# The value matmuls of a block issued as two halves of 256 columns, one behind every two pairs of scores

## The reference

```
xn = layernorm(x)                         # x: 2 x 2048 x 256
q, k, v = split(xn @ w_qkv.T)             # 16 heads of 16
q, k = rope(q), rope(k)
attn = softmax(q @ k.T / 4)               # 2048 x 2048 for each of 32 batch and head
s = (attn @ v) @ w_out.T
g = silu(expert_ffn(xn))                  # each token to one of 8 experts
out = x + s * g
```

## Time and profile before

| | |
|---|---|
| time, median of 3 runs | 1651.2 us (1650.79 to 1651.39) |
| the profiled execution | 1654.93 us, its span 1653.2 us |
| mean granted TensorE clock | 0.976 |
| TensorE matmul busy | 1539.2 us, 93% |
| VectorE busy | 1367.1 us, 83% |
| ScalarE busy | 1189.0 us, 72% |
| GpSimd busy | 141.1 us, 9% |

### The profile page before, as it was taken

One profiled execution on the slowest core, in us unless ns is written; L12 is line 12 of the kernel. 1 busy time (PEld: TensorE's weight loads), 2 busy tenths in 40 slices (PEclk: granted clock), 3 DMA queues, 4 the chain that ended last, 5 costly groups with the idle time before them and its releaser, 6 DMA issues.

```text
span 1653.2 us, 29704 instructions
## 1 busy us (share of the span) xinstructions
PE 1539.2 (93%) x9121; PEld 660.2 (40%) x9121; DVE 1367.1 (83%) x1563; ACT 1189.0 (72%) x2381; POOL 141.1 (9%) x160
## 2 busy tenths in 40 slices
PE   6897999989899999999999999999999999999998
PEld 4453333346433333333333333333333333333336
DVE  7678799964599999999999999999999999999705
ACT  4452377855677787787788778778777877877780
POOL 2232322100122100000010000000010000000100
PEclk9998599989899999999999999999999999999999
DMA  5673234425444324222222242222222422222303
GB/s 199 226 193 117 55 78 100 67 48 154 103 78 78 61 42 93 42 42 42 39 40 41 39 90 39 39 41 41 41 42 42 90 39 39 41 40 35 62 4 118
DMA packets 77820, 116.54 MB, mean 70 GB/s; under 512 B 29072, under 2 KB 64272, under 8 KB 70800
## 3 DMA queue, kind: packets, MB, share of 16 engines
q1 hardware_dynamic: 69632, 101.89, 31.9%
q0 software_dynamic: 3072, 8.39, 2.0%
q10 hardware_dynamic: 5072, 5.72, 1.0%
HBM read 75.31 MB, written 39.85 MB: 70 GB/s over the span
## 4 chain that ended last, share of the span: by engine, by line
PE 74%; ACT 17%; DVE 3%; issue 3%; DMA 2%; SPq 1%; ACTq 0%; POOLq 0%; DVEq 0%
PE ps L1114 31%; PE ps L1103 31%; ACT arena L582 16%; PE ps L1035 3%; PE ps L1193 2%; PE ps L1036 1%; PE ps L1094 1%; PE ps L1209 1%; PE ps L1239 1%; DVE arena L692 1%; PE ps L1059 1%; DMA arena<-xs_d 1%; PE ps L1166 1%; PE ps L1046 1%; DMA out<-arena 1%
## 5 line engine op out<-in xcount | busy, mean ns | idle before, releaser
L726 DVE TENSOR_REDUCE arena<-ps 128x1 f32<-128x1024 f32 x992 | 1174.1, 1219 | 127.3 <-PE ps L1094 119.2
L582 ACT ACTIVATE arena<-ps 128x512 f32<-128x512 f32 x2048 | 1059.7, 603 | 275.3 <-PE ps L1103 274.1
L1103 PE MATMUL ps<-qs,ks 50*128 50x512 f32 x2048 | 754.5, 449 | 61.0 <-ACT arena L582 29.5
L1094 PE MATMUL ps<-ks,qs 48*128 48x512 f32 x1984 | 796.3, 474 | 4.3 <-DVE arena L726 2.5
L1103 PEld LDWEIGHTS ps<-qs,ks 50*128 50x128 f32 x2048 | 341.9, 186 | 685.6 <-issue 436.2
L1114 PE MATMUL ps<-arena 128*32 128x512 f32 x4096 | 551.6, 611 | 0.8 <-ACT arena L582 0.8
L1094 PEld LDWEIGHTS ps<-ks,qs 48*128 48x128 f32 x1984 | 331.9, 187 | 48.0 <-DVE arena L726 17.0
L1114 PEld LDWEIGHTS ps<-arena 128*32 128x32 f32 x4096 | 80.9, 108 | 130.3 <-ACT arena L582 113.7
L969 POOL COPY arena<-v_sb 128x256 f32 (+1 forms) x32 | 13.3, 416 | 1108.1 <-ACT arena L574 1090.8
L1035 PE MATMUL ps<-arena 128*128 128x512 f32 x128 | 68.8, 620 | 0.7 <-ACT arena L496 0.7
L692 DVE TENSOR_REDUCE arena<-ps 128x1 f32<-128x1024 f32 x32 | 39.1, 1222 | 23.8 <-PE ps L1059 23.8
(11 more groups left out here) (103 smaller groups left out, 543.0 us busy)
## 6 DMA issues: line engine op xcount, KB each, us to landing
qs<-parts_d SPq DMA_DIRECT2D x186, 128.0 KB
ks<-parts_d SPq DMA_DIRECT2D x186, 128.0 KB
parts_d<-arena SPq DMA_DIRECT2D x64, 256.0 KB, 2.6
xs_d<-arena SPq DMA_DIRECT2D x13, 384.0 KB, 3.4
arena<-xs_d SPq DMA_DIRECT2D x13, 384.0 KB, 3.8
ys_d<-arena SPq DMA_DIRECT2D x13, 384.0 KB, 2.8
onum_d<-arena SPq DMA_DIRECT2D x128, 32.0 KB
out<-arena ACTq DMA_DIRECT2D x16, 256.0 KB, 2.1
```

Of the source, the lines that this page charges most:

```text
L582: nc.scalar.activation(prob[kb % 2][:, c * W:(c + 1) * W], ps[:, bank, :], ACT.Exp, scale=SCALE).then_inc(exp_done[bank], 1)
L726: nc.vector.tensor_reduce(most[head_slot][:, tile, u:u + 1], ps[:, AB + 2 * u:AB + 2 + 2 * u, :], AX.XY, ALU.max).then_inc(a_reduced[u], 1)
L1094: ins = nc.tensor.matmul(ps[:, AB + c, :], qs[head_slot][ABASE:ABASE + KR, tile * P:(tile + 1) * P].bitcast(F32R), ks[head_slot][ABASE:ABA ...
L1103: nc.tensor.matmul(ps[:, bank, :], ks[s][0:KS, kb * P:(kb + 1) * P].bitcast(F32R), qs[s][0:KS, c * W:(c + 1) * W].bitcast(F32R), start=Tru ...
```

## The change

The value group is issued in two halves: columns 0 to 255 of all four column groups, then columns 256 to 511. A block is now: B scores c = 0 and 1 of the next block with their A scores, first half of the values of this block, B scores c = 2 and 3 of the next block with their A scores, second half. So score c = 3 moves from the start of its own block to the block before. The first half waits for all of the block's exponentials. `pv_done` is given by the second half. The wait for the next head's loads stands ahead of score c = 0 of block 15. All four scores of the very first block are issued ahead. Ahead of the expert part one score (c = 3 of the next head) is held back and issued behind it; for this pair 1 is written out on its own behind a loop that holds only pair 0.

```
--- before.py
+++ after.py
@@ -1103,18 +1103,21 @@
                 nc.tensor.matmul(ps[:, bank, :], ks[s][0:KS, kb * P:(kb + 1) * P].bitcast(F32R),
                                  qs[s][0:KS, c * W:(c + 1) * W].bitcast(F32R), start=True, stop=True).then_inc(scored[bank], 1)
 
-            def weigh_values(pi, s, kb):
-
-                if kb == 0:
+            def weigh_values(pi, s, kb, half):
+
+                if kb == 0 and half == 0:
                     pe.wait_ge(v_staged[s], pi + 1)
                     pe.wait_ge(o_out[1 - s], past(pi + s))
-                for c in range(1, QT):
-                    pe.wait_ge(exp_done[b_bank(s, kb, c)], past(b_before(pi, s, kb, c) + 1))
+                if half == 0:
+                    for c in range(1, QT):
+                        pe.wait_ge(exp_done[b_bank(s, kb, c)], past(b_before(pi, s, kb, c) + 1))
+                lo, hi = half * W // 2, (half + 1) * W // 2
                 for c in range(QT):
-                    last = nc.tensor.matmul(ps[32 * c:32 * (c + 1), PVB, :], vst[s][:, kb, :],
-                                            prob[kb % 2][:, c * W:(c + 1) * W],
-                                            start=(kb == 0), stop=(kb == KB - 1))
-                last.then_inc(pv_done[kb % 2], 1)
+                    last = nc.tensor.matmul(ps[32 * c:32 * (c + 1), PVB, lo:hi], vst[s][:, kb, :],
+                                            prob[kb % 2][:, c * W + lo:c * W + hi],
+                                            start=(kb == 0 and half == 0), stop=(kb == KB - 1 and half == 1))
+                if half:
+                    last.then_inc(pv_done[kb % 2], 1)
 
             pe.wait_ge(pt_out, NT)
             pe.wait_ge(qkv_out, NT)
@@ -1129,12 +1132,13 @@
             pe.wait_ge(counts_out, 1)
             pe.wait_ge(loaded[0], 16 * LOADS)
             pe.wait_ge(shift_loaded[0], 64)
-            for c in range(QT - 1):
+            for c in range(QT):
                 score(0, 0, 0, c)
 
-            def pair(pi, last_pair):
+            def pair(pi, last_pair, hold=False):
                 for s in range(2):
                     for kb in range(KB):
+                        held_back = hold and s == 1 and kb == KB - 1
                         g = pi * (2 * KB) + (s * KB + kb)
                         ahead = kb + AHEAD - KB
                         with_a = not last_pair or (s == 0 and ahead < KB)
@@ -1143,17 +1147,16 @@
                         b_slot, b_pi = (s, pi) if kb < KB - 1 else (1 - s, pi + s)
                         if with_a and ahead % KB == 0:
                             pe.wait_ge(a_loaded[a_slot], (pi + 2) * (16 * LOADS))
+                        if with_b and kb == KB - 1:
+                            pe.wait_ge(loaded[b_slot], (pi + 1 + s) * (16 * LOADS))
+                            pe.wait_ge(shift_loaded[b_slot], (pi + 1 + s) * 64)
                         for c in range(QT):
-                            if c == 0:
-                                score(pi, s, kb, QT - 1)
-                            elif with_b:
-                                if c == 1 and kb == KB - 1:
-                                    pe.wait_ge(loaded[b_slot], (pi + 1 + s) * (16 * LOADS))
-                                    pe.wait_ge(shift_loaded[b_slot], (pi + 1 + s) * 64)
-                                score(b_pi, b_slot, (kb + 1) % KB, c - 1)
+                            if with_b and not (held_back and c == QT - 1):
+                                score(b_pi, b_slot, (kb + 1) % KB, c)
                             if with_a:
                                 score_a(g + AHEAD, a_slot, ahead % KB, c)
-                        weigh_values(pi, s, kb)
+                            if c % 2:
+                                weigh_values(pi, s, kb, c // 2)
 
             def turn_sorted(i):
 
@@ -1212,9 +1215,11 @@
                 pe.wait_ge(inter_out, NF)
                 pe.wait_ge(y_out, NF)
 
-            with pe.Fori(0, FB) as pi:
+            with pe.Fori(0, FB - 1) as pi:
                 pair(pi, False)
+            pair(FB - 1, False, hold=True)
             experts()
+            score(FB, 0, 0, QT - 1)
             with pe.Fori(FB, NP - 1) as pi:
                 pair(pi, False)
             pair(NP - 1, True)
```

## The result

The changed kernel takes 1763.2 us (median; its runs lie between 1758.2 and 1798.8) against 1651.3: ratio 1.070, 95% interval 1.063 to 1.077. The forecast was 1596 us, with a range of 1582 to 1642. The profiled execution is the longest, 1798.8 us, 36 us over the median, so what it shows as the price of a stall is more than the median run pays.

The account below looks back on a forecast made before the run. A latency loop through TensorE and ScalarE was taken as the bound. Saving 60.2 us over 16 pairs, net 55.5, takes the profiled execution from 1654.93 to 1599.4 us; the median, 3.7 lower, is 1596, range 1582 to 1642.

Parts of the forecast that it names:

- What bounded the kernel before: Attention block: a closed wait loop of score, exponential, score and value group through TensorE and ScalarE, 2.61 us per block.
- The new block: Attention block after the change: TensorE itself the bound, 2 x (0.66 + 0.57) = 2.47 us for 2.61, 0.145 us less.
- the slower rival: Value half groups: a fixed cost per short pass, bare weight load of 0.11 us each, 113 us, 1708 us; chance 0.11.
- the 60 cycles: Value matmuls: if each costs this much, 8 further records add 0.20 us per block, sum near 1700 us; argued against.
- The end of a head: First block of the next head: half group waits for the exponential queued behind ScalarE's copy, +0.65 us in each head.
- The sum: Whole kernel: 3.76 us less per pair of heads, 60.2 us in 16 pairs, net 55.5 us after deductions.
- the rival of the instruction memory: TensorE's loop over pairs: body grows from 5 blocks to 7 and may not stay, so jumps back wait; chance 0.17.
- The rival's price: Twelve jumps back of the loop: 2.1 us each or twice that, 25 to 50 us, so 1621 to 1646 us.
- the half-clock blocks: Some nine attention blocks at half clock, where TensorE already is the bound: 9 x (0.15 + 0.3) = 4 us off the gain.

Follow-up runs that it names:

- Experiment 6: Also a_whole: score c=3 moved into the block before as in the change, but the value group left whole behind all four scores; 1689.8 us, one execution.
- experiment 7: Changed kernel with 110 padding instructions, ScalarE's copy of a head's sums put behind exponential c=3 instead of between c=2 and c=3; 1591.9 us, ratio 0.965.
- experiments 2 to 5: Changed kernel with 110 or 200 padding instructions: 1608.0, 1741.0 us; kernel before with waits behind each value group, without or with 128 more ahead: 1922.0, 1990.3 us.
- a_pad110: Changed kernel with 110 instructions of satisfied waits ahead of TensorE's first work, moving the second loop from 8 blocks to 7; 1608.0 us, ratio 0.972.
- experiments 3 and 4: Kernel before, old matmul order, with 16 instructions of satisfied waits behind each value group, the second with 128 more at the start; 1922.0 and 1990.3 us.
- Experiment 8: Changed kernel with 210 padding instructions and whole value groups in the first ten blocks behind the experts; 1623.1 us, ratio 0.986.
- experiment 4: Kernel before with 16 instructions of satisfied waits behind each value group and 128 more ahead of TensorE's first work; 1990.3 us, one execution.
- 9: Changed kernel with the copy behind exponential c=3 and 95 padding instructions in place of 110; 1592.5 us, ratio 0.966.
- a_straight: Changed kernel with TensorE's two loops over pairs of heads written out, no jump, other engines unchanged; 1609.4 us, ratio 0.970.

## Why the prediction was wrong, point by point

- **What bounded the kernel before** was right: the loop score, exponential, score, value group. Experiment 6 leaves it in place and stays at 2.61 to 2.67 us; with the halves it is gone.
- **The new block** was right. 2 x (0.66 + 0.57) = 2.47 forecast, 2 x 1.23 measured; the first pass of a half group lasts 403 ns, the shortest second ones 376, as taken from the earlier trace rows. So the slower rival by a fixed cost per short pass fell. With it fell my reading of the 60 cycles that the Trainium skill, "TensorEngine Tiling (Array Packing)", Instruction Overhead, gives for each matmul: as a cost of every further record they don't show here, where 8 further records in a block cost nothing that can be seen.
- **The end of a head** was right: 0.69 us for 0.65, caused as said (experiment 7 removes two thirds of it by moving the copy alone). Heads of 40.15 and 40.51 for 40.14 and 40.34. (The terms of the sum add up to 55.8 us, not to the 55.5 written; that changes nothing.)
- **The sum failed at the step that took the loop's jumps as free**, that is, in weighing the rival of the instruction memory at 0.17. I compared the body, "from 5 blocks to 7", with eight. The body is 6.6 blocks long, and what counts is how many it touches: 8, since it begins at 0.73 of one. With one block fetched ahead, 7 touched blocks stay and 8 don't, if eight are held. That is the size that the Trainium skill, "Runtime: NRT & Kernel Launch", Instruction fetch mechanics, gives, and the placements of experiments 2 to 5 agree (7 blocks at 21.16 and 15.04, and at 5.04: no fetch in the loop; 8 blocks at 20.73, 21.51, 15.54 and 4.54: a fetch and a stall at the jump). Length and place both follow from the program.
- **The rival's price was mis-sized.** I gave 2.1 to 4.2 us per jump and 1621 to 1646 us in all. The stall at the jump is 3.8 to 5.6, 4.90 in the chain shown, where 0.55 follows at the next block. Behind it comes half clock, which I had left out although showed what it does to a value group: a half block takes 2.16 us at 1.2 GHz (1541.40 to 1543.56 above, where no A scores are left; with them the changed kernel has the same 2.16, from 1016.10 to 1018.26) for 1.23. 28.7 us of half clock hold 6.6 blocks, which cost 6.6 x 1.86 = 12 us more than at full clock. 12 + 5.5 makes 17, measured 56.50 - 40.15 = 16.35 in the head above, which had 27.3 us of it. Twelve of them are 196 us, and the forecast for a profiled execution, 1599.4, with 196 makes 1796; measured 1798.8. That is the profiled, longest run. By the medians a jump costs (1763.2 - 1608.0)/12 = 13 us.
- **The last 12 us.** a_pad110 has 1608 for 1596. Some 3 us are the padding's (its first half clock comes at 67 us, not at 64). Half clock behind the experts lasted 47.8 us in its profile, against 10.2 before; 37.6 us more, at 1.86 us lost in each 4.32, are 16 us in that execution. The stretch from 159 us on was 14 us shorter than before and gives some of it back. I had taken the half-clock blocks over unchanged in number.

**What stays open** is why the clock often takes longer to come back with half groups. Behind a stretch without work (experts or a jump) it took 10.2, 13.7 and 10.2 us with whole groups behind the experts (before, and the kernels of experiments 3 and 4), 6.8 in experiments 6 and 8, and 6.8 at every jump of experiment 4. With half groups it took 17.1 to 47.8 behind the experts (eight kernels), and 6.8 to 47.8 at jumps. Two other places speak against a rule that long stretches belong to the half groups. The one that starts at 154 to 171 us, ahead of the first heads, lasts 30.7 to 47.8 us with whole groups (four kernels) and 34.1 to 58.0 with half ones. And in the last pair whole groups have the longest of all: 61.4 us in experiment 6, and 81.9 in both kernels of experiments 3 and 4 (the windows view of the first):

```profile
1807.00:1887.00 80.00, 79.22 (x237) 25.57 (x230) 0.25 (x1) 39.65 (x76) 0.00 (x0) 0.50 0.01 2
```

Experiment 8's profile fits an effect of the order, its runs don't confirm it, and the mechanism wasn't tried. The spread of some 15 us between runs of the best versions isn't settled either.

The best version is experiment 7, or 9: the change, the loop placed in 7 blocks, and the copy one exponential later, 1592 us, 3.5% under the kernel before. It rests on the count of instructions ahead of the loop, and any edit there can undo it.

## What to carry to other kernels

Count the instructions of a hardware loop's body and their place, whenever an edit adds instructions to it; here the loop was free as long as it touched 7 blocks of 256 on TensorE, and cost 10 to 16 us a jump at 8 (6 in the old order of matmuls). Look in the profile for instruction packets during a loop: there should be none. And price an idle stretch of TensorE by what the clock does behind it, not by its own length: in the changed kernel's profile the first was twice the second.

## What the runs showed of the hardware

- TensorE's instruction memory held a loop over 7 blocks of 16 KB, and lost its start at 8. Once it was lost, all of the body was fetched anew in each pass (9 packets), of which only the first ones were waited for. In a straight program 106 packets cost 0.1 us in a pair of heads of 80.7.
- A jump to a block that was gone stopped TensorE for 3.2 to 5.6 us (37 jumps in four kernels, some with the old order and some with the new), and for 7.1 to 7.4 in the kernel whose loop is twice as long.
- The clock fell to 1.2 GHz behind such a stop each time. It also fell in the last pair of heads behind short waits, of 0.72 us with half groups (a_straight) and 0.62 us with whole ones (a_whole), and stayed there for 64.9 and 61.4 us with TensorE busy throughout. For a_straight:

```profile
1541.00:1606.00 65.00, 65.00 (x311) 21.66 (x310) 0.25 (x1) 32.05 (x59) 0.00 (x0) 0.51 0.01 2
```
